# The spectral layer moved into the second attention of an eight-layer transformer kernel, one group of rows per attention unit

## The reference, cut to what matters

```python
x = x + jnp.tanh(g_xattn[1]) * _L1_xattn_ref(_layernorm(x, axis=-1), ctx_768, ...)
x = x + jnp.tanh(g_ffn[1]) * _L1_ffn_ref(_layernorm(x, axis=-1), w_freq_real, w_freq_imag, bias)

def _L1_xattn_ref(x, context, Wq, Wk, Wv, Wo, bo):     # 8 heads of 64, 64 keys a sequence
    q, k, v = heads(x @ Wq), heads(context @ Wk), heads(context @ Wv)
    attn = softmax(einsum('bhsd,bhld->bhsl', q, k) * scale)
    return merge(einsum('bhsl,bhld->bhsd', attn, v)) @ Wo + bo

def _L1_ffn_ref(x, w_freq_real, w_freq_imag, bias):
    y_freq = einsum('bnd,do->bno', fft(x, axis=-1), w)
    return real(ifft(y_freq, axis=-1)) + bias
```

## Time and profile before

| | |
|---|---|
| median of 3 runs | 3093.61 us (3089.88 to 3094.95) |
| the profiled execution | 3090.51 us, span 3088.5 us |
| granted TensorE clock, mean over the span | 0.976 |
| busy TensorE, VectorE, ScalarE, GpSimd | 94%, 72%, 51%, 38% |
| DMA | 69 GB/s on average |

### The profile page before, as it was taken

How to read it: one execution, slowest core, us unless ns; L and a number is a source line. 1 busy time by engine, 2 the same in 40 slices (tenths; PEclk the granted TensorE clock), 3 DMA queues, 4 the chain that set the end, 5 groups by cost and what they waited for, 6 DMA issues and landing times. The chain is left out here.

```text
span 3088.5 us, 89570 instructions
## 1 busy us (share of the span) xinstructions
PE 2907.3 (94%) x34642; PEld 2271.6 (74%) x34642; DVE 2219.8 (72%) x5750; ACT 1577.6 (51%) x2906; POOL 1181.7 (38%) x1274
## 2 busy tenths in 40 slices
PE   7999799999998999869997999999998999999978
PEld 6888545555556888747776888888886888888854
DVE  6777566666654666668887777788766788888756
ACT  6777312111113777537774333333335777777756
POOL 6677200000003777554540000000004677777753
PEclk9999899999998999979998999999998999999999
DMA  5000165666551000011111333333330000000001
GB/s 158 19 10 8 62 195 175 184 181 186 168 168 35 12 10 10 2 53 26 26 25 57 111 103 104 105 96 97 106 111 16 12 10 10 8 10 10 10 1 55
DMA packets 110871, 212.03 MB, mean 69 GB/s; under 512 B 18737, under 2 KB 30449, under 8 KB 110194
## 3 DMA queue, kind: packets, MB, share of 16 engines
q1 hardware_dynamic: 110194, 209.03, 22.5%
q10 hardware_dynamic: 512, 0.92, 0.1%
HBM read 198.34 MB, written 5.77 MB: 66 GB/s over the span
## 5 line engine op out<-in xcount | busy, mean ns | idle before, releaser
L341 PE MATMUL ps<-parts 128*128 128x512 f32 (+3 forms) x1568 | 624.2, 398 | 32.9 <-DVE parts L955 18.8
L342 PE MATMUL ps<-parts 128*128 128x512 f32 (+3 forms) x1568 | 565.2, 360 | 0.0
L343 PE MATMUL ps<-parts 128*128 128x512 f32 (+3 forms) x1568 | 563.2, 359 | 0.0
L311 POOL TENSOR_TENSOR rstd<-mv,eps 128x4 f32<-128x4 f32 x112 | 23.2, 207 | 1205.1 <-DVE mv L294 1204.9
L1878 ACT ACTIVATE work<-ps 128x512 f32<-128x512 f32 x272 | 162.3, 597 | 442.1 <-PE ps L343 442.0
L341 PEld LDWEIGHTS ps<-parts 128*128 128x128 f32 (+2 forms) x1568 | 299.7, 191 | 104.7 <-ACT work L790 26.2
L537 POOL TENSOR_TENSOR work<-work 128x512 f32<-128x512 f32 x256 | 267.5, 1045 | 276.7 <-DVE work L925 276.7
L343 PEld LDWEIGHTS ps<-parts 128*128 128x128 f32 (+2 forms) x1568 | 298.7, 191 | 46.2
L342 PEld LDWEIGHTS ps<-parts 128*128 128x128 f32 (+2 forms) x1568 | 301.3, 192 | 20.2
L1843 PEld LDWEIGHTS ps<-early,work 128*128 128x128 f32 x2176 | 281.4, 192 | 18.9 <-DVE pause L1932 0.3
L1843 PE MATMUL ps<-early,work 128*128 128x128 f32 x2176 | 287.9, 276 | 0.1
(11 more groups left out here) (284 smaller groups left out, 6083.7 us busy)
## 6 DMA issues: line engine op xcount, KB each, us to landing
work<-gate_rows SPq DMA_DIRECT2D x128, 512.0 KB, 5.5
work<-expert_rows SPq DMA_DIRECT2D x512, 128.0 KB, 2.9
work<-gate_rows SPq DMA_DIRECT2D x128, 256.0 KB, 6.6
work<-in_ctxT SPq DMA_DIRECT2D x72, 192.0 KB, 2.4
out<-x SPq DMA_DIRECT2D x16, 256.0 KB, 2.3
work<-work SPq DMA_DIRECT2D x224, 16.0 KB
work<-work SPq DMA_DIRECT2D x16, 128.0 KB, 2.3
early<-in_l0f_w SPq DMA_DIRECT2D x1, 1536.0 KB
```

Of the source, the lines that this page charges most:

```text
L341: T.matmul(out, lh, rh, start=True, stop=False)
L342: T.matmul(out, lh, rl, start=False, stop=False)
L343: return T.matmul(out, ll, rh, start=False, stop=True)
```

## The change

`spectral` goes away. In the second attention (`spec` is true for it alone) group k - 1 goes through the spectral layer while the attention works on unit k: VectorE takes the moments (`x_moments_of`) in step 0; GpSimd works out the reciprocal deviation and minus the mean times it (`x_deviation`) in step 1; ScalarE normalises the rows, x * rstd + shift, with four instructions that read a scale and a bias column (`x_scale`), at the end of step 1; TensorE turns them (`x_turn`) in step 2 and ScalarE copies them (`take_x`); TensorE multiplies them by G (`x_mix`) and VectorE adds them to x with the gate as one instruction (`x_add`) in step 3; GpSimd adds the bias (`x_bias`) in step 0 of the unit after. The turned rows and the product lie in the halves that `attend`'s two PSUM banks 5 and 6 leave free. Group 15 is done behind the last unit. `gc` is no longer made. The work area of layer 2 grows by 384 columns.

```diff
+    if spec:
+        xn, xT = w([TG, P]), w([GT])
+        xst, xmv, xrstd, xshift = w([TG, 6]), w([TG, 2]), w([TG]), w([TG])
+        ps_x = c.ps[:, 5:7, NJ * S:512]
...
+            def x_deviation(g):
+
+                pool.wait_ge(x_moments, g + 1)
+                need(pool, x_ready, g)
+                G.tensor_tensor(xshift, c.zero[:, 0:TG], xmv[:, :, 0], ALU.subtract)
+                G.tensor_tensor(xrstd, xmv[:, :, 1], c.w["eps"][:, 0:TG], ALU.add).then_inc(x_eps, 1)
+                pool.wait_ge(x_eps, g + 1)
+                G.tensor_tensor(xrstd, xrstd, c.w["half"][:, 0:TG], ALU.pow).then_inc(x_rstd, 1)
+                pool.wait_ge(x_rstd, g + 1)
+                G.tensor_tensor(xshift, xshift, xrstd, ALU.mult).then_inc(x_shift, 1)
+
+            def x_bias(g):
+                pool.wait_ge(x_added, g + 1)
+                G.tensor_tensor(norm.xg(g), norm.xg(g), bc(c.w["rows"][:, 2, :], 1, TG), ALU.add).then_inc(x_biased, 1)
...
+                        if spec and t == 1 and has_prior(it, u):
+                            x_deviation(un.k - 1)
...
+                        if spec and t == 0 and has_second_prior(it):
+                            x_bias(un.k - 2)
...
+            def x_turn(g):
+
+                te.wait_ge(x_ready, g + 1)
+                for t in range(TG):
+                    last = T.transpose(ps_x[:, t // 2, t % 2 * P:(t % 2 + 1) * P], xn[:, t, :], c.w["ident"][:, :])
+                last.then_inc(x_turned, 1)
+
+            def x_mix(g):
+
+                te.wait_ge(x_out, g + 1)
+                for t in range(TG):
+                    last = T.matmul(ps_x[:, t // 2, t % 2 * D:(t % 2 + 1) * D], xT[:, t * P:(t + 1) * P], c.w["l1f_g"][:, :], start=True, stop=True)
+                last.then_inc(x_mixed, 1)
...
+                if spec and t == 3 and has_prior(it, u):
+                    te.wait_ge(x_out, un.k)
+                if spec and t == 0 and has_second_prior(it):
+                    te.wait_ge(x_added, un.k - 1)
                 attend(t)
...
+                if spec and t == 2 and has_prior(it, u):
+                    te.wait_ge(ot_out, n + 1)
+                    x_turn(un.k - 1)
+                if spec and t == 3 and has_prior(it, u):
+                    te.wait_ge(ot_out, n + 1)
+                    x_mix(un.k - 1)
...
+            def x_scale(g):
+
+                act.wait_ge(x_shift, g + 1)
+                need(act, x_turned, g)
+                for t in range(TG):
+                    src = c.w["x"][:, bass.ds(g * TG + t, 1), :][:, 0, :]
+                    last = A.activation(xn[:, t, :], src, ACT.Identity, bias=xshift[:, t:t + 1], scale=xrstd[:, t:t + 1])
+                last.then_inc(x_ready, 1)
+
+            def take_x(g):
+                act.wait_ge(x_turned, g + 1)
+                A.activation(xT.rearrange("p (b k) -> p b k", b=2), ps_x, ACT.Copy).then_inc(x_out, 1)
...
+                        if spec and t == 2 and has_prior(it, u):
+                            take_x(un.k - 1)
                         if not (end and t == TG - 1):
                             take_values(n + 1, t + 1, value_bank(t))
...
+                        if spec and t == 1 and has_prior(it, u):
+                            x_scale(un.k - 1)
...
+                        if spec and t == 0 and has_prior(it, u):
+                            x_moments_of(un.k - 1)
+                        if spec and t == 3 and has_prior(it, u):
+                            x_add(un.k - 1)
...
-            elif layer == 3:
-                spectral(c, d)
```

More of the change, by code:

```diff
@@ L394, in wide_attention @@
     null = layer == 3
+    spec = layer == 1
     masked = layer in (0, 3)
@@ L447, in wide_attention @@
     acc_out, edges = sem("acc_out"), sem("edges")
+    if spec:
+        x_turned, x_out, x_mixed, x_added, x_bn, x_moments, x_eps, x_rstd, x_shift, x_ready, x_biased = (
+            sem(n) for n in ("xt", "xt_out", "mixed", "x_added", "x_bn", "x_moments", "x_eps", "x_rstd", "x_shift", "x_ready", "x_biased"))
     fin_bn, fin_mv, fin_eps, fin_rstd, fin_y, fin_yg = (
@@ L474, in turns, with has_prior, has_second_prior @@
         return t == 1 and not last and (u == 0 or not null)
+    def has_prior(it, u):
+        return u == 1 or not (isinstance(it, int) and it == 0)
+    def has_second_prior(it):
+        return not (isinstance(it, int) and it == 0)
     first = Unit(0, 0, passes)
@@ L613, in _ @@
             by_twos_and_last(pool, units // 2, body)
+            if spec:
+                x_bias(units - 2), x_deviation(units - 1), x_bias(units - 1)
             if null:
@@ L775, in _ @@
             project(units * TG - 1, Unit(units // 2 - 1, 1, passes), TG - 1)
+            if spec:
+                te.wait_ge(x_added, units - 1)
+                x_turn(units - 1), x_mix(units - 1)
         @block.scalar
@@ L896, in _ @@
             by_twos(act, units // 2, body)
+            if spec:
+                x_scale(units - 1), take_x(units - 1)
             if null:
@@ L932, in add, with x_moments_of, x_add @@
                                        op0=ALU.mult, op1=ALU.add).then_inc(added, 1)
+            def x_moments_of(g):
+                ve.wait_ge(added, g + 1)
+                V.memset(c.pause[:, 1:2], 0.0)
+                for t in range(TG):
+                    last = V.bn_stats(xst[:, t, :], c.w["x"][:, bass.ds(g * TG + t, 1), :][:, 0, :])
+                last.then_inc(x_bn, 1)
+                ve.wait_ge(x_bn, g + 1)
+                V.memset(c.pause[:, 0:1], 0.0)
+                for t in range(TG):
+                    last = V.bn_aggr(xmv[:, t, :], xst[:, t, :])
+                last.then_inc(x_moments, 1)
+            def x_add(g):
+                xg = norm.xg(g)
+                ve.wait_ge(x_mixed, g + 1)
+                V.scalar_tensor_tensor(out=xg.rearrange("p (b t) c -> p b t c", b=2), in0=ps_x.rearrange("p b (t c) -> p b t c", c=D),
+                                       scalar=c.w["tg"][:, 5:6], in1=xg.rearrange("p (b t) c -> p b t c", b=2),
+                                       op0=ALU.mult, op1=ALU.add).then_inc(x_added, 1)
             def finish_moments(g):
@@ L1043, in _ @@
                 add(c.ngroup - 1)
+                if spec:
+                    x_moments_of(units - 1), x_add(units - 1)
 def narrow_attention(c, d):
@@ L1448, in by_pairs @@
     body(n - 1, 1, True)
[L1451 to L1553, removed]
@@ L2538, in program @@
         for layer in layers:
+            if layer == 3:
+                continue
             parts = {0: 8 * GT + 12 * P * 2 + 24 * D, 2: 8 * GT + 12 * P * 2 + 24 * D, 5: 4 * GT + 4 * W2N, 6: 6 * GT + 12 * P * 2 + 48 * D}
-            c.open_work({0: 15 * 1024, 2: 15 * 1024, 6: 14 * 1024, 5: 12 * 1024}.get(layer, 26 * 1024), parts.get(layer, 0))
+            c.open_work({0: 15 * 1024, 2: 15 * 1024 + 384, 6: 14 * 1024, 5: 12 * 1024}.get(layer, 26 * 1024), parts.get(layer, 0))
             if layer in (0, 2, 6):
```

## The result

The changed kernel takes 3116.56 us (median of 4 runs, 3114.76 to 3119.1) against 3091.86 us for the kernel before (median of 4, in the same comparison): a ratio of 1.0079, 95% interval 1.0066 to 1.0092. It is slower by 24.7 us. The profiled execution has a span of 3113.0 us, against 3088.5.

The account below looks back on a forecast made before the run. TensorE, busy 94% of the span, was taken as the bound. Units growing 4.29 us each, 62.4 us in all, against 37.8 us removed give a loss of 24.6 us on about 3092: 3117 us, range 3093 to 3140.

Parts of the forecast that it names:

- rival 1: The forecast itself: each unit of the second attention grows by 3.9 to 4.8 us, 3111 to 3125 us; chance 0.50.
- The tail: Group 15 alone after the attention's last addition: 10.5 us left of 48.3, so 37.8 removed, 36.0 at worst.
- TensorE's own work: Per unit, four transposes (x_turn) and four fp32 multiplications (x_mix) on TensorE: 1.34 us together.
- The handoffs: Steps 2 and 3: x_turn and x_mix wait for ScalarE's copy of the result, 0.4 us each, 0.8 a unit.
- The turn: Step 1: x_bias beside norm.scale delays it, so TensorE's transposes of the next group wait 0.35 us a unit.
- ScalarE: Steps 1 to 2: x_scale between exponentials and pt_out is fully exposed, so TensorE waits 1.8 us before attend.
- break-even: Unit growth at which the change neither gains nor loses: 37.8 us removed over 15 units, 2.5 us a unit.
- Rival 4: One more wait a unit, from late GpSimd scale_probs or TensorE's clock falling: 1.5 us more, 3140 us; chance 0.18.
- Rival 2: Milder, still slower: x_shift in time, x_scale takes 1.1 us, unit grows 3.1 us, about 3100 us; chance 0.17.
- rival 3: Not slower: ScalarE's delay does not reach TensorE, unit grows 1.34 to 2.5 us, 3074 to 3092 us; chance 0.15.

Follow-up runs that it names:

- experiment 8: Changed kernel with ScalarE copying raw rows in step 0, VectorE scaling at the addition, x_turn and x_mix behind the value job, x_bias in step 3: 3068.59 us.
- Experiment 1: Changed kernel with x_turn and x_mix behind the value job of their step and take_x behind take_values: 3105.62 us.
- experiment 2: Changed kernel with x_bias in step 3 behind spread instead of step 0 behind the split: 3105.07 us.
- experiment 3: Changed kernel with x_scale's four instructions as plain copies without scale and bias columns, rows not normalised: 3098.2 us.
- experiment 4: Changed kernel with x_scale's four instructions done twice, the first four into a spare tile: 3164.57 us.
- experiment 9: Changed kernel with raw rows copied instead of x_scale, x_turn, x_mix and x_bias left where the change has them: 3081.06 us.

## Why the prediction was right

The forecast was 3117 us and 24.6 us of loss; measured were 3116.56 and 24.7. Each wait that the forecast priced was there, in its place and with the releaser it named. That the sum came out to half a microsecond is luck: a unit was forecast to grow by 4.29 us and grew by 3.75 at the full clock, which is below the 3.9 to 4.8 that the forecast gave itself (rival 1). Those 8 us too many were made up by costs that the sum did not have: the clock's falls (4.5), a last unit that grew by 6.05 where about 3.3 were reckoned, and a longer tail (1.6).

- **The tail.** Forecast 10.5 us, 36.0 of gain at worst; measured 12.1 and 36.2. The lower clock, which the text kept as a bound, was the case: x_turn took 1.09 and x_mix 2.07, 1.4 us more than the terms for them. There are six handoffs and not five, but they took 0.4 us together instead of 0.75.
- **TensorE's own work**, 1.34: measured 1.4 (0.44 and 0.95), as the whole growth of the unit in experiment 8.
- **The handoffs**, 0.8: about 0.6 by the steps of the unit (step 2 grew by 2.38 us, of which 1.65 is attend's and 0.44 x_turn; step 3 by about 1.25, of which 0.95 is x_mix). Experiment 1 took 0.46 back.
- **The turn**, 0.35: measured 0.2. Its cause, x_bias in the way of norm.scale, is shown by experiment 2.
- **ScalarE**, 1.8: measured 1.65. Its length of 1.6 was right to 0.05 (four instructions at 483 ns, where 456 was reckoned), and the wait for x_shift cost 0.2. That it is exposed in full is shown by experiments 3 and 4: 0.74 us less and 1.5 us more of it changed the unit by as much. That it decides, with the break-even at 2.5 us a unit, is shown by experiment 9, whose unit is 1.98 us longer than before.
- **What was left out** is TensorE's clock. Rival 4 had it as a price of 1.5 us a unit; it came in three units (4.5 us) and in the last one, which was to save 1 us and grew by 6.05 (14.57 to 20.62), 2.3 us more than a steady unit. Fifteen units of 3.75 with these, less 0.4 in the first and 0.7 in the last but one, are the 62.1 us, where 62.4 were forecast from 4.29 without them. The forecast argued against a fall with a unit that has TensorE 82% busy. By its own terms, 3 us idle in 24, that is 88%, and the trace has 90% (21.16 of 23.41 us). The clock fell all the same, so the argument from the busy share did not hold.

Rival 2 (x_shift in time, short instructions) and rival 3 (ScalarE's delay covered) are out by the 1.66 us before attend. Of rival 4, the part on GpSimd's late scale_probs is out, since no transposes waited for it in the steady units; the part on the clock came true in three units of the first fourteen.

## What to carry to other kernels

Work that is moved under a saturated engine is free only where the engine that takes it has idle time at that very place: ScalarE was idle a quarter of the unit, but not between the exponentials and the copy that attend waits for. With 1.65 us a unit there the kernel lost 25 us; with that place left free (experiment 9) it gained 12.6, of which 4.6 lie in the tail. Before giving such work a place, read what the next instruction of that queue feeds. The cure that worked here was to make the work independent of the late chain (raw rows, scaled at the end): one instruction that waits for nothing late could stand in a gap of ScalarE in step 0. The same four instructions at another place in ScalarE's order were not tried.

## What the runs showed of the hardware

TensorE's granted clock fell to the lower level behind an idle time before attend of 1.65 to 1.73 us in three of the first 14 units, in the changed kernel and in experiment 1 alike. With 1.33 us in each unit (experiment 2) it fell in none of the 14, and with 2.6 to 3.3 (experiment 4) in twelve. A fall in the changed kernel made its unit 1.5 us longer, on top of the wait itself. These are counts of one execution each, and in the last unit the falls did not follow the gap before attend.

Four TENSOR_SCALAR of VectorE took 1.12 us alone, 2.19 beside one instruction of GpSimd and 3.46 beside three in a row. Each GpSimd instruction held up one of them for about its own length, also where that one is recorded as starting 0.04 or 0.07 us ahead (1127.68 against 1127.72, 1103.88 against 1103.95).
